# Biases of an expert layer loaded per block with the weights, in an attention and mixture-of-experts kernel

## The reference

```
x = x + attention(layernorm(x))        # 16 heads of 64, causal linear attention with cos/sin weights, bias on q, k, v and output
x = x + moe(layernorm(x))
moe(y): logits = y @ gate_w                       # 8 experts
        top 2 of the logits, softmax over the two -> combine[t, e]
        h = gelu(y @ w1[e] + b1[e])               # 128 -> 512
        out = sum over e of combine[t, e] * (h @ w2[e] + b2[e])     # 512 -> 128
```

## Time and profile before

| what | value |
|---|---|
| median of 3 runs | 384.93 us (384.72 to 385.65) |
| profiled execution, its own time | 386.15 us |
| span of the profiled execution | 384.3 us |
| PE busy | 353.2 us, 92% |
| PEld (weight loads) busy | 320.9 us, 83% |
| DVE / ACT / POOL busy | 236.3 / 158.9 / 130.4 us |
| HBM read, written | 22.63 MB, 15.47 MB |
| issues of w1b and of yb | 39 and 39 |

### The profile page before, as it was taken

One profiled execution on the slowest core, in us unless ns is written; L12 is line 12 of the kernel. 1 busy time (PEld: TensorE's weight loads), 2 busy tenths in 40 slices (PEclk: granted clock), 3 DMA queues, 4 the chain that ended last, 5 costly groups with the idle time before them and its releaser, 6 DMA issues.

```text
span 384.3 us, 10812 instructions
## 1 busy us (share of the span) xinstructions
PE 353.2 (92%) x4167; PEld 320.9 (83%) x4167; DVE 236.3 (61%) x677; ACT 158.9 (41%) x374; POOL 130.4 (34%) x132
## 2 busy tenths in 40 slices
PE   0899999999999999999999999999999999999910
PEld 0677999988899988889999888999799999999910
DVE  4689864668886466797646678875646433222205
ACT  2575232267323136732322673122245455666600
POOL 5013241103058310304840130352326755555520
PEclk9999999999999999999999999999999999999975
DMA  7741332334001000000100001700463557877439
GB/s 250 197 185 63 147 143 107 131 124 159 2 31 33 25 9 3 0 2 26 40 25 9 2 0 31 206 25 20 115 172 109 163 142 211 231 200 205 124 83 244
DMA packets 32753, 38.35 MB, mean 100 GB/s; under 512 B 4115, under 2 KB 25008, under 8 KB 31680
## 3 DMA queue, kind: packets, MB, share of 16 engines
q1 hardware_dynamic: 27232, 31.62, 27.2%
q0 software_dynamic: 2272, 4.46, 3.3%
q10 hardware_dynamic: 3200, 1.58, 1.6%
HBM read 22.63 MB, written 15.47 MB: 99 GB/s over the span
## 4 chain that ended last, share of the span: by engine, by line
PE 79%; DMA 6%; DVE 6%; issue 3%; POOL 3%; SPq 1%; ACTq 0%; ACT 0%; POOLq 0%; DVEq 0%
PE ps L1211 8%; PE ps L1173 8%; PE ps L1404 7%; PE ps L1389 7%; PE ps L1190 7%; PE ps L1218 7%; PE ps L1247 7%; PE ps L1085 6%; PE ps L1087 6%; PE ps L1086 6%; PE ps L1238 4%; PE ps L1130 3%; DMA zin<-zbuf 2%; DMA yb<-ybuf 2%; POOL ybuf L480 2%
## 5 line engine op out<-in xcount | busy, mean ns | idle before, releaser
L615 ACT ACTIVATE os<-ps 128x260 f32<-128x260 f32 x64 | 24.8, 388 | 100.5 <-PE ps L1218 100.5
L656 ACT ACTIVATE hT<-ps,b1t 128x128 f32<-128x128 f32 x156 | 44.5, 368 | 34.8 <-PE ps L1389 34.0
L480 POOL DMA_INDIRECT ybuf<-yr,slot x32 | 31.7, 991 | 72.8 <-issue 37.4
L438 POOL TENSOR_TENSOR on<-tcs,rden 128x1024 f32<-128x1024 f32 x16 | 30.4, 1901 | 64.8 <-DVE rden L801 64.8
L518 POOL DMA_INDIRECT zbuf<-z,yb x39 | 37.9, 972 | 30.3 <-DVE z L1020 26.3
L788 DVE TENSOR_TENSOR state<-ps,state 128x260 f32<-128x260 f32 x64 | 27.4, 428 | 31.4 <-ACT os L615 29.1
L778 DVE TENSOR_TENSOR am<-ps,pair 128x1024 f32<-128x1024 f32 x32 | 38.7, 1210 | 9.9 <-issue 6.6
L1020 DVE TENSOR_SCALAR z<-ps,yb 128x128 f32<-128x128 f32 x39 | 13.7, 351 | 47.2 <-PE ps L1404 47.2
L1404 PE MATMUL ps<-w_sb,hT 128*128 x312 | 41.7, 277 | 0.8 <-DVE z L1020 0.8
L1211 PE MATMUL ps<-vcs,am 128*64 128x65 f32 x1024 | 42.2, 225 | 0.0
L1389 PE MATMUL ps<-xb,w1b 128*128 128x128 f32 x312 | 41.2, 276 | 0.0
(11 more groups left out here) (136 smaller groups left out, 619.6 us busy)
## 6 DMA issues: line engine op xcount, KB each, us to landing
w1b<-in_L_ffn_w SPq DMA_DIRECT2D x39, 256.0 KB, 3.1
ybuf<-blank SPq DMA_DIRECT2D x8, 1152.0 KB, 4.6
yb<-ybuf SPq DMA_DIRECT2D x39, 72.0 KB, 3.0
w_sb<-in_L_ffn_w SPq DMA_DIRECT2D x8, 256.0 KB, 4.6
x_sb<-in_L_attn_x SPq DMA_DIRECT2D x4, 256.0 KB, 5.2
pair<-c_pair SPq DMA_DIRECT2D x16, 64.0 KB, 2.0
zin<-zbuf SPq DMA_DIRECT2D x4, 256.0 KB, 5.6
zin<-zbuf ACTq DMA_DIRECT2D x4, 256.0 KB, 6.1
```

The costliest lines, as they stand in the source:

```text
L480: pool.indirect_dma_start(ybuf, bass.IndirectOffsetOnAxis(ap=slot[:, k, c:c + 1], axis=0), yr[:, k, c, :], None).then_inc(y_out[u], 16)
L656: act.activation(hT[:, b % 2, f, :], ps[:, b % 2 * 2 + f // 2, f % 2 * P:f % 2 * P + P], ACT.Gelu, bias=b1t[:, f, b:b + 1]).then_inc(h_ok, 1)
```

## The change

- b1 is laid behind w1 on the host: a weight row has 516 floats, 512 of w1 and 4 bias columns, and ScalarE's Gelu takes its bias from those columns of `w1b`.
- Each block has a third load on SP, b2 of its expert, one row of 512 B broadcast to 128 partitions, on the same semaphore as the weights. TensorE's hidden product waits for both.
- The weight load of block b waits for VectorE's add of block b-6 (`zs_ok`) instead of TensorE's hidden products of block b-6.
- `weighed` is two operations: add b2 to PSUM, then multiply. TensorE's next down product waits for the add alone.
- The gate is one float32 product per chunk in place of three float32r ones; `yT_lo`, `gate_hi` and `gate_lo` go.
- combine, turn_comb, comb_turned, biases, open_sum, the b1 products of the tables, eight b1 loads, the single b2 load and two memsets go.

The core of the diff:

```diff
@@ SP
-            sp.wait_ge(memsets, 2)
-            sp.dma_start(b2_sb[0:E, :], b2).then_inc(c_in, 16)
...
-            for e in range(E):
-                sp.dma_start(b1q[e * QC // E:(e + 1) * QC // E, :], b1[e:e + 1, :].broadcast_to([QC // E, F])
-                             ).then_inc(b1_in, 16)
...
                 if b >= WR:
-                    sp.wait_ge(h_ps, 2 * (b - WR) + 2)
+                    sp.wait_ge(zs_ok, b - WR + 1)
                 sp.dma_start(w1b[b % WR][:], w1[bass.ds(at // PITCH, 1), :, :].rearrange("e p n -> p (e n)")
+                             ).then_inc(w1_in[b % WR], 16)
+                sp.dma_start(b2b[:, b % WR, :], b2[bass.ds(at // PITCH, 1), :].broadcast_to([P, D])
                              ).then_inc(w1_in[b % WR], 16)
@@ POOL
-            pool.memset(b2_sb[:], 0.0).then_inc(memsets, 1)
-            pool.memset(combT[:], 0.0).then_inc(memsets, 1)
@@ ACT
-            act.wait_ge(row_in, 16 * 3)
-            act.activation(gate_hi[:], gate_sb[:], ACT.Copy).then_inc(whi_ok, 1)
...
-                act.activation(yT_hi[:, 0:n], ps[:, bank, 0:n], ACT.Copy).then_inc(yThi_ok, 1)
+                act.activation(yT[:, 0:n], ps[:, bank, 0:n], ACT.Copy).then_inc(yT_ok, 1)
...
-                                   bias=b1t[:, f, b:b + 1]).then_inc(h_ok, 1)
+                                   bias=w1b[b % WR][:, F + f:F + f + 1]).then_inc(h_ok, 1)
@@ DVE
-            def y_low(u, bank=6):
...
-            def combine(i):
...
-                dve.tensor_copy(b1t[:, :, at:at + n], ps[:, bank, 352:352 + FB * n].rearrange("p (b n) -> p b n", n=n))
...
-            def open_sum(i, bank=7):
...
                 dve.wait_ge(z_ps, b + 1)
+                dve.tensor_tensor(zs[:, b % 2, :], ps[:, 4, 0:D], b2b[:, b % WR, :], ALU.add).then_inc(zs_ok, 1)
                 if b >= ZR:
                     dve.wait_ge(z_out[b % ZR], 16 * (b // ZR))
-                dve.tensor_scalar(z[:, b % ZR, :], ps[:, 4, 0:D], yb[b % YR][:, D + 1:D + 2], None, ALU.mult
+                dve.wait_ge(zs_ok, b + 1)
+                dve.tensor_scalar(z[:, b % ZR, :], zs[:, b % 2, :], yb[b % YR][:, D + 1:D + 2], None, ALU.mult
                                   ).then_inc(z_ok, 1)
@@ PE
-                pe.wait_ge(yThi_ok, u + 1)
-                pe.wait_ge(yTlo_ok, u + 1)
+                pe.wait_ge(yT_ok, u + 1)
+                pe.wait_ge(row_in, 16 * 3)
                 for c in range(len(UNITS[u][1])):
-                    last = split3(ps[:, bank, c * E:(c + 1) * E], (yT_hi, yT_lo), (gate_hi, gate_lo),
-                                  lambda t: t[:, c * P:(c + 1) * P], lambda t: t[:])
+                    last = mm(ps[:, bank, c * E:(c + 1) * E], yT[:, c * P:(c + 1) * P], gate_sb[:], start=True, stop=True,
+                              skip_group_check=True)
...
-            def turn_comb(i):
...
-            def biases(i):
...
-                for f in range(FB):
-                    mm(ps[:, bank, 352 + f * n:352 + (f + 1) * n], b1q[:, f * P:(f + 1) * P], match[:, 0:n],
-                       start=True, stop=True, skip_group_check=True)
...
-                pe.wait_ge(w1_in[b % WR], 16 * (b // WR) + 16)
+                pe.wait_ge(w1_in[b % WR], 32 * (b // WR) + 32)
...
-                    pe.wait_ge(z_ok, b)
+                    pe.wait_ge(zs_ok, b)
@@ host
+def with_bias_columns(w, b):
+    columns = b.reshape(E, FB, P).transpose(0, 2, 1)
+    return np.ascontiguousarray(np.concatenate([w, columns], axis=2))
```

More of the change, by code:

```diff
@@ L147, in moe_block @@
         yr = sb("yr", [P, 2, SC, ROW])
-        yT_hi = sb("yT_hi", [P, ST], F32R)
-        yT_lo = sb("yT_lo", [P, ST], F32R)
+        yT = sb("yT", [P, ST])
         lg = sb("lg", [P, SC, E])
@@ L170, in moe_block @@
         match = sb("match", [QC, NB])
-        b1t = sb("b1t", [P, FB, NB])
         tab = sb("tab", [1, 2, NB], I32)
-        comb = sb("comb", [P, SC, E])
-        combT = sb("combT", [P, SC, P])
         yb = [sb(f"yb{k}", [P, ROW]) for k in range(3)]
-        w1b = [sb(f"w1b{k}", [P, F]) for k in range(2)]
+        w1b = [sb(f"w1b{k}", [P, F + FB]) for k in range(2)]
+        b2b = sb("b2b", [P, WR, D])
+        zs = sb("zs", [P, 2, D])
         xb = sb("xb", [P, XR, P])
@@ L197, in moe_block @@
         w2_sb = sb("w2_sb", [P, E, F])
-        w1b += [sb(f"w1b{k}", [P, F]) for k in range(2, WR)]
+        w1b += [sb(f"w1b{k}", [P, F + FB]) for k in range(2, WR)]
         zin = sb("zin", [P, 2, NC, D])
@@ L269, in moe_block @@
         yT_ps = sem("yT_ps")
-        yThi_ok = sem("yThi_ok")
-        yTlo_ok = sem("yTlo_ok")
+        yT_ok = sem("yT_ok")
         lg_ps = sem("lg_ps")
@@ L350, in blank_next @@
                              blank[:].rearrange("p s w -> p (s w)")).then_inc(blank_out, 16)
-            sp.wait_ge(memsets, 6)
+            sp.wait_ge(memsets, 4)
             for e in range(2):
@@ L427, in _ @@
             pool.memset(blank[:], 0.0).then_inc(memsets, 1)
-            pool.wait_ge(memsets, 5)
+            pool.wait_ge(memsets, 3)
             pool.memset(blank[:, :, D:D + 1].bitcast(U32), 0xFFFF).then_inc(memsets, 1)
@@ L500, in attention @@
                         if i == 0:
-                            pool.wait_ge(c_in, 16 * 4)
+                            pool.wait_ge(c_in, 16 * 3)
                         open_residual(i)
@@ L582, in front @@
                         y_turned(i - 1, 6)
-                    if i >= 2 and j == COMB_AT:
-                        comb_turned(i - 2)
                 keys(K_JOBS - 1)
@@ L599, in x_turned @@
                 act.activation(xT_hi[:], ps[:, 6, :], ACT.Copy).then_inc(xThi_ok, 1)
[L601 to L606, removed]
             def out_sums(i, n):
@@ L747, in front @@
                         if not tail:
-                            dve.wait_ge(c_in, 16 * 4)
+                            dve.wait_ge(c_in, 16 * 3)
                         masked(i, 0)
@@ L762, in front @@
                         normed2(i - 1)
[L763 to L766, removed]
                     if tail and m == BEST_AFTER:
@@ L981, in attention @@
                         shares(i - 1)
-                        combine(i - 1)
                     if i == NS - 1 and p == 2:
@@ L995, in _ @@
             front(0, False)
-            dve.wait_ge(memsets, 4)
+            dve.wait_ge(memsets, 2)
             attention(0, False)
@@ L1070, in _ @@
                 weighed(b)
[L1071 to L1076, removed]
             for k in range(NS):
@@ L1440, in _ @@
             step(9)
[L1441 to L1445, removed]
-            turn_comb(NS - 1)
-            step(12)
-            biases(NS - 1)
-            for b in range(13, NB):
+            for b in range(10, NB):
                 step(b)
 _INS = ["L0_attn_x", "L0_attn_Wq", "L0_attn_bq", "L0_attn_Wk", "L0_attn_bk", "L0_attn_Wv", "L0_attn_bv",
-        "L0_attn_Wo", "L0_attn_bo", "L0_ffn_gate_w", "L0_ffn_w1", "L0_ffn_b1", "L0_ffn_w2", "L0_ffn_b2"]
+        "L0_attn_Wo", "L0_attn_bo", "L0_ffn_gate_w", "L0_ffn_w1", "L0_ffn_w2", "L0_ffn_b2"]
 def shape_constants():
@@ L1500 @@
         arrays[f"in_{name}"] = heads_in_blocks(arrays[f"in_{name}"])
+    arrays["in_L0_ffn_w1"] = with_bias_columns(arrays["in_L0_ffn_w1"], inputs["L0_ffn_b1"])
     arrays.update(shape_constants())
```

39 lines of the change are left out of this document (4 added, 35 removed).

## The result

The changed kernel takes 392.83 us (390.19 to 395.01, four runs) against 384.93 for the kernel before on the same chip (three runs; a fourth took 914.58 us and is left out): ratio 1.0206, 95% interval 1.0153 to 1.0258. That is slower, and inside the range of 384 to 394, but about 7.9 us slower where 4.2 was forecast. All four runs lie above the 389.1 of the forecast, and the median is 0.4 above the forecast's own range of 386.0 to 392.4. The profiled execution took 393.36 with a span of 391.6 (before 386.15 and 384.3), so its spans differ by 7.3.

The account below looks back on a forecast made before the run. TensorE bounds the kernel before the loop, and SP's queue becomes the loop's bound. Loop +7.8, earlier start -4.0 and last add +0.35 give +4.2 on 384.9: 389.1 us, own range 386.0 to 392.4, with some rivals 384.0 to 394.0.

Parts of the forecast that it names:

- TensorE ahead of the loop: Before the block loop, dropped transposes, b1 and b2 products and the shorter gate take 4.78 us off the path.
- The 0.2 for the late routing: VectorE's new add lies open before the late routing that shares VectorE, costing 0.2 us.
- Rival 5: In the gate, an f32 product takes four records' time, 1.77 instead of 0.95 us per unit: 391.6 us; chance 0.05.
- The issue price: On SP's queue in the loop, the third load costs 0.54 us, making a block 2.21 against TensorE's 1.90.
- Rival 1: SP takes the third issue in its stride; TensorE or the results' chain bounds: -4.5, 380.4 us; chance 0.13.
- rival 2: Gain and loss cancel with an issue of 0.36 us on SP: -0.3, 384.6 us; chance 0.07.
- rival 3: DMA engines become the bound in the loop, with landings of 4.9 instead of 3.0: 395.5 us; chance 0.1.
- block 13's row load "keeps its place": On SP's queue it stays at 308.53 in old times, held by block 3's result scatter; 4.0 is taken off later.
- The loop from block 17 to 38: SP's row loads: 21 x 2.21 us plus four longer issues totalling 2.2, putting block 38 at 366.2 instead of 356.22.
- Landing: Block 38's rows land 3.0 us after issue, the last transpose comes 0.2 behind, at 369.4 against 361.62.
- The ring: Weight loads waiting for the add of block b-6 cost nothing in the loop; as a rival binding, chance 0.02.
- The marks named in advance: Three SP issues per 2.2 us block, TensorE idle 6 to 9 us, loop starting and ending some 4 us earlier and later.

Follow-up runs that it names:

- experiment 5: The kernel before with only the gate changed to one f32 product per chunk: 383.22 us, ratio 0.9957.
- experiment 1: The changed kernel with b2 laid behind each weight row on the host, same bytes, no third load: 384.09 us, ratio 0.9968.
- experiment 4: The kernel before with only a third load per block added, b2's row broadcast to a tile nobody reads: 398.83 us, ratio 1.0355.
- Experiment 11: b2 in the weight rows, rows of blocks 0 and 1 loaded before their weights, 16 row buffers instead of 10: 375.96 us, ratio 0.9777 to before.
- the folded kernel: The changed kernel with b2 in the weight rows and no third load: 384.09 us; with rows of blocks 0 and 1 loaded first, 381.19 us.
- the square: Four kernels: third issue with 64 KB a block 392.83 us, with 8 KB 390.25; no third issue with 64 KB 384.09, with b2 loaded once 382.51.
- experiment 6: The changed kernel with the weight load waiting for Gelu of block b-6 and only the b2 load for the add: 392.37 us, ratio 1.0177.
- experiment 3: The changed kernel with the b2 load issued twice, four issues per block: 430.37 us, ratio 1.1174.
- experiment 9: The changed kernel with expert 0's b2 loaded once for every block, no third load per block: 382.51 us, ratio 0.9938.

## Why the prediction was right, and which terms were off

*TensorE ahead of the loop: right, a little too small.* The first rows came 4.69 earlier, forecast 4.23 (4.78 less 0.55). The difference is the gate but for 0.04, 0.52 a unit for the 0.38 booked in three units. The 0.2 for the late routing doesn't show: the scatter before block 13 is 4.7 earlier too. The eight records were there, but at 0.10 each rather than 0.11 to 0.125. Rival 5 would have had 1.77 against a measured 0.81; experiment 5 excludes it. The Trainium skill ("FP8 and Floating Point Precision", TensorE Precision Notes) counts four passes for true FP32. Here a float32 product is two records of 0.10, so a pass doesn't have the price of a record.

*The issue price: right.* 0.51 measured, 0.54 taken; the cycle 2.18 for 2.21. Rival 1 and rival 2 (an issue of 0.37 or less) fall with it. The total alone would not tell: 392.8 lies between the forecast (389.1) and rival 3 (395.5). The marks do: the wait is the one for rows and not for weights, the rows land after 3.2 and not 4.9, and the DMA share is 0.74 and not 0.9. The Trainium skill ("DMA: Bandwidth & Descriptors", Issuing engines are not separate DMA queues) has the sequencer's time for an issue as usually small beside the transfer. It is so here, 0.51 to a landing of 3.2, and it decides all the same, since the transfers overlap and the issues don't.

*The step that failed: block 13's row load "keeps its place", on a path taken as 4.0 earlier.* It came only 2.6 earlier, at 305.92. It waits for a scattered result, and that landed later after its issue, by the chain of waits, after, then before, then in experiment 1:

```profile
300.81 4.37 DMA zbuf<-z,yb
```

```profile
305.55 2.24 DMA zbuf<-z,yb
```

```profile
303.72 4.30 DMA zbuf<-z,yb
```

The scatter was issued 4.7 earlier, 0.7 more than forecast, but took 2.1 longer and landed 2.6 earlier: 1.4 us missing. Why it took 4.37 stays open. It isn't the third load by itself: experiment 1, which has none, shows 4.30, and experiment 4, the kernel before with the third load, 3.30. In all three it was issued 1.1 to 1.3 us behind block 12's row load, in the kernel before 2.9 behind it; no run here tested that distance. Experiment 11 shows, in the folded kernel, that the waits for scattered results mattered.

*The loop from block 17 to 38: mis-sized.* 49.65 measured (315.16 to 364.81) for 48.6. The regular part was 21 x 2.18 = 45.8 and the long pieces 3.9, booked at 2.2. "Four in this stretch, at 0.56" took the mean of five old ones; the three longest here (0.81, 1.15, 1.29) have 2.3 over 0.33 between them, and the other 1.6 lies for the most part in steps between the issues that are longer by 0.1 to 0.5. With the slightly shorter cycle (2.18 for 2.21) that makes +1.0. From block 13 to 17 it is +0.2.

*Landing.* "The rows land 3.0 later": the last transpose came 3.68 behind the issue of its rows, 3.2 booked, +0.5. The bytes of the third load, which the sum had at nothing, cost 1.6 to 2.6 in the square, with the noise named there. Behind the last transpose all went as booked, +0.4.

Together 1.4 + 0.2 + 1.0 + 0.5 = 3.1, which is the 7.3 of the profiled spans less 4.2. The largest part, 1.4, has no explanation.

*The ring:* right, nothing but one early wait, by SP's waits (under experiment 6). *The marks named in advance:* three issues per block at 2.2, yes; TensorE released by the rows, 16 times and 10.9 us in all, where 6 to 9 were named; the loop some 4 earlier at its start, yes; its end 6.9 later, not 4.

## What to carry to other kernels

Count the issues per iteration on the queue that feeds a loop like instructions of an engine: an added DMA cost its 0.51 us of issue here whether it carried 8 KB or 64, and where the queue has less slack than that (0.23 us of 1.90 here), small per-iteration data belongs in a transfer that is made anyway. When such a fix returns less than its sum, look for the next late input, here the order of the first loads and the ring of row buffers; with the fold they turned a loss of 2% into a gain of 2%. And subtract starts, not lengths, for short products.

## What was not expected of the hardware

- After some waits of TensorE of 1.7 to 3.6 us the granted clock stood at 0.50 (1.2 GHz of 2.4) for two to six microseconds, so that a late load costs more than its wait. It happened in experiments 1, 3, 4 and 9. In experiment 9 it fell behind 0.25 + 1.40, in experiment 6 it didn't behind 0.25 + 1.44, so the length of the wait alone doesn't decide.
- Costs beside a saturated issue queue aren't additive: a fourth load cost 37.5 (experiment 3) where 25 issues of 0.48 make 12, with landings from 3.2 to 5.0.
- An issue of 0.33 sometimes takes 0.8 to 1.8. In the changed kernel there was one at 344.49 (1.15), and the DMA queues between 342 and 347 show an instruction fetch in the same stretch:

```profile
q8 instruction: 1, 0.02, 1.2%
```

A coincidence in time, seen at other long issues too; no run here tested it.
